# Macaron block on one Trainium2 core: the w2 products of the first expert pass move between two units of a projected tile

## The chip, the cores and the metric

One core of one Trainium2 chip. The metric is the device time of one execution in microseconds (us). The kernel before took 2403.8 us, the median of 3 runs (2402.45 to 2406.37).

## The reference

x has 8 batches of 1024 tokens of width 512. The block is a feed-forward half, an attention and the same feed-forward half again:

```
x = x + 0.5 * ffn(layernorm(x))
x = x + attn(layernorm(x))
x = x + 0.5 * ffn(layernorm(x))
```

ffn: 32 experts with a hidden width of 2048. Every expert picks 8 tokens of each batch by its gate weights and merges them into one row per batch, so an expert sees only 8 rows:

```
merged = einsum('bked,bke->bed', tok, vals)
h = gelu(concat([merged, 1]) @ w1[e])      # 512+1 -> 2048
o = concat([h, 1]) @ w2[e]                 # 2048+1 -> 512
out.at[flat_idx].add(einsum('beo,bke->bkeo', o, vals))
```

attn: q, k, v are projections of the normalised x by Wq, Wk, Wv (512 x 512 each); exp(q) and exp(k) enter a linear attention with running sums over the sequence, and Wo projects the result. All is float32. One expert has 8 MB of weights, so a pass over 32 experts reads some 270 MB.

## The kernel before, in words

Each engine has an instruction stream of its own, written out by hand, and they meet in semaphores: `wait_ge` stands ahead of the instruction that needs something, `then_inc` behind the one that gives it. The stages are: the gate over 64 tiles of 128 tokens (`gate_*`), the first expert pass (`experts_*` with p = 0), the attention (`attention_*`), the second expert pass (p = 1), and the final scatter.

**The first expert pass** does two things. For each expert e, TensorE (`experts_pe`, L733) runs the products with w1 (L738 to L746, into PSUM bank 0), transposes the result (L762 to L765, bank 1), and runs the products with w2 (L775 to L783, bank 4 or 5). Each weight matrix comes as two chunks of 2 MB: chunks 4e and 4e+1 are w1, 4e+2 and 4e+3 are w2. The products are thin (32 columns of stationary data, four side by side). Between them TensorE computes the projections of q, k and v of the first x ahead of the attention (`ahead_pe`, L918): tile 2e-1 behind the w1 products, tile 2e behind the transposes. A tile has three **units** (q, k, v), each 12 products of 128x512 into bank 2 or 3 in turn; the values are split in two parts (XTH, XTL and WTH, WTL), so one unit is 4 x 3 products. A unit may start when the unit two before it has been read out of its bank: q and k by ScalarE (L950, semaphore `s_pea`), v by VectorE (L959, `s_ped`). Every fourth expert TensorE also runs `scatter_pe` (two products) behind the w1 products.

**From transposes to w2 products.** VectorE adds the bias to the transposed values (L842, `s_hb`), ScalarE applies the gelu (L814, `s_ht`), and the w2 products wait for `s_ht` (L773). In `experts_act` (L800) the order for an expert is: copy of the w1 result (L806), `ahead_act` of tile 2e-1, gelu, `ahead_act` of tile 2e; every fourth expert then copies the sum of four experts from bank 4 or 5 (L826, `s_pt`), which `scatter_pe` waits for. `ahead_act` (L941) splits the next tile (L909), stores the tile before (`store_act`, L936, 768 KB to p_scratch on ScalarE's DMA queue), and reads the q and the k unit out of their banks. In `experts_dve` (L831) the order is the eviction of the v unit of tile 2e-1 (L959), the bias (L842), the split of the next tile (L915), the v unit of tile 2e.

**The weights** come through SyncE's queue (`experts_sp`, L715; `load_chunk`, L671). In the first pass they have four slots in SBUF, one for each chunk of an expert (`slot_of`, L239). The load of chunk g+4 waits until the products have used chunk g (`s_used`, raised behind the products at L746 and L783), and SyncE issues in the order of the chunks. Behind the four loads of every even expert it issues one load of 1 MB of xt_scratch (`load_xg`, L705), which holds the values that the projections read.

The first expert has an order of its own: its tile 0 is projected behind its w2 products (L785). In the second pass there are eight slots and no projections.

Of the kernel before, what the change touches and what calls it, by code (L numbers as in the profile page):

```python
# [20 lines left out]
def macaron_block(nc, x, Wq, bq, Wk, bk, Wv, bv, Wo, bo, gate_w, gate_b, w1, w2, out):  # L21
# [21 lines left out]
    with ctx:  # L43
# [195 lines left out]
        def slot_of(g):  # L239
            return g % 4 if g < 4 * E else (4, 5, 6, 7, 2, 0, 1, 3)[g % 8]  # L240
# [55 lines left out]
        def mm(o, l, r, start, stop):  # L296
            return nc.tensor.matmul(o, l, r, start=start, stop=stop, skip_group_check=True)  # L297
# [435 lines left out]
        def experts_pe(pe, p):  # L733
            pe.wait_ge(s_mg, 8 * p + 8)
            for e in range(E):
                x, g = E * p + e, 4 * (E * p + e)
                pe.wait_ge(s_hg, x)
                for kt in range(4):  # L738
                    h = g + kt // 2
                    v = ring[slot_of(h)].rearrange("p (k n) -> p k n", k=2)  # L740
                    pe.wait_ge(d_ring[slot_of(h)], 16 * turn[h])
                    for j in range(4):
                        t = mm(ps[32 * j:32 * j + 32, 0, :], MG[:, kt, 8 * e:8 * e + 32],
                               v[:, kt % 2, 512 * j:512 * j + 512], kt == 0, kt == 3)
                    if kt % 2 == 1:
                        t.then_inc(s_used, 1)  # L746
                if e == 0:
                    pe.wait_ge(d_b1, 64 * p + 64)
                    for q in range(4):
                        t = nc.tensor.transpose(ps[:, 1, 128 * q:128 * q + 128],  # L750
                                                BS.rearrange("p (c t) -> p t c", t=4)[:, q, :], IDN[:, :])
                    t.then_inc(s_btT, 1)
                if e % 4 == 0 and e:
                    scatter_pe(pe, p, e // 4 - 1)
                if p == 0 and e == 0:
                    weights_pe(pe, 2, 8)
                if p == 0 and e:
                    ahead_pe(pe, 2 * e - 1)
                pe.wait_ge(s_hg, x + 1)
                pe.wait_ge(s_hb, x)  # L760
                pe.wait_ge(s_bt, p + 1)
                for q in range(4):  # L762
                    t = nc.tensor.transpose(ps[:, 1, 128 * q:128 * q + 128],  # L763
                                            HG[e % 2].rearrange("p (c t) -> p t c", t=4)[:, q, :], IDN[:, :])
                t.then_inc(s_htT, 1)  # L765
                if p == 0 and e == 0:
                    weights_pe(pe, 8, 16)
                    bias_pe(pe)
                if p == 0 and e:
                    ahead_pe(pe, 2 * e)  # L770
                if e % 4 == 0:
                    pe.wait_ge(s_pt, x // 4 - 1)
                pe.wait_ge(s_ht, x + 1)  # L773
                k = 4 + e // 4 % 2
                for j in range(4):  # L775
                    h = g + 2 + j // 2
                    v = ring[slot_of(h)].rearrange("p (j i n) -> p j i n", j=2, i=4)
                    pe.wait_ge(d_ring[slot_of(h)], 16 * turn[h])
                    for q in range(4):
                        t = mm(ps[32 * q:32 * q + 32, k, :], HT[e % 4][:, 128 * q + 32 * j:128 * q + 32 * j + 32],  # L780
                               v[:, j % 2, q, :], e % 4 == 0 and j == 0, e % 4 == 3 and j == 3)
                    if j % 2 == 1:
                        t.then_inc(s_used, 1)  # L783
                if p == 0 and e == 0:
                    ahead_pe(pe, 0)  # L785
                if p == 1 and 1 <= e < 3:
                    rank_pe(pe, e - 1)
            scatter_pe(pe, p, 7)
            if p == 0:
                ahead_pe(pe, NT - 1)  # L790

        def scatter_pe(pe, p, G):
            pe.wait_ge(s_selc, 17)
            pe.wait_ge(s_pt, 8 * p + G + 1)
            for half in range(2):
                off = 128 * half + 28 - 4 * G
                t = mm(ps[:, 6 + half, :], SEL[:, off:off + 128], PT[G % 2], G == 0, G == 7)
            t.then_inc(s_sel, 1)
# [65 lines left out]
        def weights_pe(pe, lo, hi):  # L864
            for u in range(lo, hi):
                m, kt = u // 4, u % 4
                pe.wait_ge(*((d_wst[m], 16) if m < 2 else (d_x0[m - 2], 32)))
                if u == 2:
                    pe.wait_ge(s_pr3, 8)
                if u == 3:  # L870
                    pe.wait_ge(s_mg, 8)
                pe.wait_ge(s_wth, u - 3)
                pe.wait_ge(s_wtl, min(u - 3, 12))
                for o in range(4):
                    t = nc.tensor.transpose(ps[:, WB[u % 4], 128 * o:128 * o + 128],
                                            WST[m][:, o, 128 * kt:128 * kt + 128], IDN[:, :])
                t.then_inc(s_wT, 1)

        def bias_pe(pe):
            pe.wait_ge(s_wth, 16)  # L880
            pe.wait_ge(d_bias, 16 * 11)
            for g in range(4):
                t = mm(ps[:, 2, :], BVT[:, g:g + 1].broadcast_to([128, 128]), WO[:, g, :], g == 0, g == 3)
            t.then_inc(s_bo, 1)
# [30 lines left out]
            tt(XTL[t % 2], XG[h % 2][:, :, 128 * (t % 4):128 * (t % 4) + 128], XTH[t % 2].bitcast(F),  # L915
               ALU.subtract).then_inc(s_xsl, 1)

        def ahead_pe(pe, t):  # L918
            if t == 0:
                pe.wait_ge(s_bo2, 1)  # L920
            pe.wait_ge(s_xsl, t + 1)
            for u in range(3):
                q = 3 * t + u
                o = q - 2
                if o >= 0:
                    if o % 3 < 2:
                        pe.wait_ge(s_pea, o // 3 * 2 + o % 3 + 1)
                    else:
                        pe.wait_ge(s_ped, o // 3 + 1)
                for j in range(4):  # L930
                    mm(ps[:, 2 + q % 2, :], XTH[t % 2][:, j, :], WTH[u][:, j, :], j == 0, False)
                    mm(ps[:, 2 + q % 2, :], XTH[t % 2][:, j, :], WTL[u][:, j, :], False, False)
                    t_ = mm(ps[:, 2 + q % 2, :], XTL[t % 2][:, j, :], WTH[u][:, j, :], False, j == 3)
                t_.then_inc(s_pu, 1)
# [490 lines left out]
        def rank_pe(pe, h):  # L1425
            pe.wait_ge(s_rank, 14)
            pe.wait_ge(s_own, 7 * h + 1)
            for i in range(2):
                t = mm(ps[:, 2 + i, :], EARLIER, PICK[:, 512 * i:512 * i + 512], True, True)
            t.then_inc(s_cnt, 1)  # L1430
# [102 lines left out]
        @block.tensor  # L1533
        def _(eng):
            pe = Engine(eng)
            gate_pe(pe)
            experts_pe(pe, 0)
            attention_pe(pe)
            experts_pe(pe, 1)
            final_pe(pe)  # L1540
# [22 lines left out]
```

## Time and profile before

| | |
|---|---|
| median of 3 runs | 2403.8 us (2402.45 to 2406.37) |
| the profiled execution's own time | 2402.62 us |
| its span, first to last instruction | 2400.9 us |
| TensorE busy | 84% of the span |
| VectorE, ScalarE, GpSimd busy | 31%, 34%, 27% |
| DMA | 762 MB, mean 317 GB/s |
| granted TensorE clock, mean | 0.921 |

The span is what the views of the trace cover; the profiled execution's own time is 1.7 us longer. The gate runs until about 140 us, the first expert pass until about 980 us, the attention until about 1740 us, the second pass until about 2370 us. In the views, PE is TensorE's matmul, SPq is SyncE's queue of DMA issues, and L297 is a helper through which nearly all matmuls go, so groups are told apart by tiles and shapes: `ps<-big 128*32 128x512` is a thin expert product, `ps<-wth,xth`, `ps<-wtl,xth` and `ps<-wth,xtl` are the projections, L763 the transposes between w1 and w2. One thin float32 product has two records, so the w1 or the w2 products of an expert are 32 records.

### The profile page before, as it was taken

To read this page: it belongs to the slowest core of one execution; us is meant where nothing else is said; L and a number is where in the kernel's file an instruction comes from. 1 tells how busy PE (TensorE), PEld (TensorE's weight loads), DVE (VectorE), ACT (ScalarE), POOL (GpSimd) and SP (SyncE) were. 2 spreads that over 40 slices of the span, in tenths; PEclk is the share of its full clock that TensorE was granted. 3 is DMA by queue.
4 is the path that set the end of the run, shared out by engine and by line. 5 is a ranking of instruction groups with operands and counts; after the bars stand their busy time and mean duration, and the time that the engine had idled before them with its cause. 6 is when DMAs were issued, how large, how long until landed. Compare 5 with 4: busy or idle time off the path is not lost.

```text
span 2400.9 us, 44276 instructions
## 1 busy us (share of the span) xinstructions
PE 2027.0 (84%) x18716; PEld 1187.7 (49%) x18716; DVE 733.1 (31%) x1229; ACT 822.0 (34%) x1539; POOL 646.4 (27%) x803
## 2 busy tenths in 40 slices
PE   5789999999999999889999999999775666666555
PEld 4556566566656665666666666666521111111111
DVE  6631111111111111266777677677420000000002
ACT  6731111111111111257777777777500000000000
POOL 8510000000000000067777777777411000000002
PEclk9899999999999999999999999999887777777888
DMA  9989999999999999654545454544399999999995
GB/s 373 339 343 368 390 403 390 384 400 380 420 400 404 392 399 386 210 212 155 160 144 168 147 157 148 164 141 159 134 400 422 425 424 424 425 424 424 425 424 212
DMA packets 130709, 762.22 MB, mean 317 GB/s; under 512 B 21156, under 2 KB 21156, under 8 KB 77264
## 3 DMA queue, kind: packets, MB, share of 16 engines
q1 hardware_dynamic: 118736, 701.35, 74.3%
q10 hardware_dynamic: 9216, 50.34, 5.0%
q0 software_dynamic: 2560, 7.70, 0.8%
q8 instruction: 149, 2.44, 0.4%
q14 instruction: 48, 0.39, 0.0%
HBM read 648.09 MB, written 105.91 MB: 314 GB/s over the span
## 4 chain that ended last, share of the span: by engine, by line
PE 44%; DMA 38%; POOL 8%; ACT 4%; issue 3%; DVE 3%; POOLq 0%; SPq 0%; ACTq 0%; DVEq 0%
PE ps L297 40%; DMA big<-in_L_ffn_w 37%; PE ps L301 3%; POOL s L1397 1%; POOL big L1394 1%; POOL big L1368 1%; POOL big L1399 1%; ACT big L1237 1%; ACT ps L1221 1%; DVE big L627 1%; POOL s L1379 1%; DVE big L305 1%; POOL big L665 1%; POOL big L1361 1%; PE ps L427 0%
## 5 line engine op out<-in xcount | busy, mean ns | idle before, releaser
L297 PE MATMUL ps<-big 128*32 128x512 f32 (+5 forms) x13776 | 1009.7, 424 | 264.8 <-DMA big<-in_L_ffn_w 233.9
L297 PEld LDWEIGHTS ps<-big 128*32 128x32 f32 (+2 forms) x13776 | 384.3, 128 | 808.7 <-issue 399.9
L305 DVE TENSOR_TENSOR big<-ps,big 128x128 f32<-128x128 f32 (+3 forms) x373 | 338.1, 932 | 749.1 <-PE ps L763 570.0
L297 PE MATMUL ps<-wth,xth 128*128 128x512 f32 x768 | 310.2, 404 | 0.0
L806 ACT COPY big<-ps 128x512 f32<-128x512 f32 x64 | 37.5, 586 | 768.5 <-PE ps L297 768.5
L297 PE MATMUL ps<-wth,xtl 128*128 128x512 f32 x768 | 300.3, 391 | 0.0
L297 PE MATMUL ps<-wtl,xth 128*128 128x512 f32 x768 | 300.3, 391 | 0.0
L1386 POOL TENSOR_SCALAR big<-big 128x1 f32<-128x1 f32 x64 | 12.2, 190 | 903.9 <-ACT ps L1221 898.6
L297 PE MATMUL ps<-wo,s 128*128 128x512 f32 x768 | 211.1, 410 | 3.4 <-ACT big L1285 1.9
L301 PE MATMUL ps<-big 128*128 128x128 f32 x1032 | 167.4, 296 | 28.6 <-ACT big L575 12.4
L950 ACT ACTIVATE big<-ps,big 128x512 f32<-128x512 f32 x128 | 88.2, 689 | 262.0 <-PE ps L297 260.1
L959 DVE TENSOR_SCALAR big<-ps,big 128x512 f32<-128x512 f32 x64 | 48.1, 751 | 425.2 <-PE ps L297 425.2
L297 PEld LDWEIGHTS ps<-wth,xth 128*128 128x128 f32 x768 | 145.7, 190 | 56.1 <-issue 27.7
L301 PEld LDWEIGHTS ps<-big 128*128 128x128 f32 x1032 | 121.6, 149 | 103.2 <-issue 60.7
L1485 POOL DMA_INDIRECT out_x<-big,idx x16 | 15.8, 987 | 553.5 <-DVE big L1479 548.7
L297 PEld LDWEIGHTS ps<-wtl,xth 128*128 128x128 f32 x768 | 145.5, 189 | 30.0 <-issue 1.9
L297 PEld LDWEIGHTS ps<-wth,xtl 128*128 128x128 f32 x768 | 144.8, 189 | 31.2
L297 PEld LDWEIGHTS ps<-wo,s 128*128 128x128 f32 x768 | 135.5, 190 | 28.3 <-ACT big L1285 3.8
L305 DVE TENSOR_TENSOR xtl<-big,xth 128x512 fp32r<-128x512 f32 x64 | 44.2, 692 | 305.6 <-ACT xth L909 305.6
L297 PE MATMUL ps<-s,tri 128*128 128x512 f32 x240 | 101.7, 471 | 11.6 <-ACT s L1246 7.0
L1394 POOL TENSOR_TENSOR big<-big 128x512 f32<-128x512 f32 x64 | 82.1, 1283 | 59.4 <-ACT big L1237 59.4
L1379 POOL TENSOR_TENSOR s<-big,s 128x512 fp32r<-128x512 f32 x64 | 82.6, 1290 | 10.4 <-ACT s L1281 4.3
(124 smaller groups left out, 1777.6 us busy)
## 6 DMA issues: line engine op xcount, KB each, us to landing
big<-in_L_ffn_w SPq DMA_DIRECT2D x256, 2048.0 KB, 22.0
p_scratch<-big ACTq DMA_DIRECT2D x64, 768.0 KB, 10.0
big<-p_scratch SPq DMA_DIRECT2D x64, 768.0 KB, 5.5
big<-in_L_attn_x SPq DMA_DIRECT2D x68, 256.0 KB, 2.9
xt_scratch<-big SPq DMA_DIRECT2D x16, 1024.0 KB, 8.2
big<-xt_scratch SPq DMA_DIRECT2D x16, 1024.0 KB, 15.5
x_weight_scratch<-big SPq DMA_DIRECT2D x64, 256.0 KB, 3.3
out_x<-big SPq DMA_DIRECT2D x64, 256.0 KB, 3.4
```

Source lines behind the costliest of these rows:

```text
L297: return nc.tensor.matmul(o, l, r, start=start, stop=stop, skip_group_check=True)
L301: t = nc.tensor.transpose(ps[:, k, 128 * j:128 * j + 128], src[:, 128 * j:128 * j + 128], IDN[:, :])
L305: return nc.vector.tensor_tensor(o, p, q, op)
L627: nc.vector.bn_stats(ST6[j], XLA[h % NX4][:, j, :]).then_inc(s_bst4, 1)
L665: nc.gpsimd.tensor_scalar(X[:, j, :], X[:, j, :], MV_[:, j, 0:1], RS_[:, j:j + 1], ALU.subtract, ALU.mult).then_inc(s_nmp, 1)
L806: nc.scalar.copy(HG[e % 2], ps[:, 0, :]).then_inc(s_hg, 1)
L950: nc.scalar.activation(PST[t % 2][:, u, :], ps[:, 2 + q % 2, :], ACT.Identity, scale=STD[:, t:t + 1]).then_inc(s_pea, 1)
L959: nc.vector.tensor_scalar(PST[t % 2][:, 2, :], ps[:, 2 + q % 2, :], STD[:, t:t + 1], None, ALU.mult).then_inc(s_ped, 1)
L1221: nc.scalar.activation(ps[:, 7, :], X1[m % 4], ACT.Square, bias=SX1[m % 2], scale=-float(D), accum_out=SQ1[m % 2]).then_inc(s_x1sq, 1)
L1237: nc.scalar.activation(PB[m % 4][:, 0, :], PB[m % 4][:, 0, :], ACT.Exp, scale=RS[m % 2]).then_inc(s_qe, 1)
L1379: nc.gpsimd.tensor_tensor(ATL, AT, ATH.bitcast(F), ALU.subtract).then_inc(s_atl, 1)
L1394: nc.gpsimd.tensor_tensor(PB[j][:, 0, :], PB[j][:, 0, :], BK, ALU.mult).then_inc(s_qb, 1)
```

## The change

Of tile 2e, whose three units stood between the transposes and the w2 products of expert e (e from 1 to 31), only the first unit (q) is left there. The second and the third (k and v) are issued behind the w2 products. Tile 2e-1, expert 0 with its tile 0, the second pass, and all other engines' streams are untouched.

```
@@ experts_pe
                 if p == 0 and e:
-                    ahead_pe(pe, 2 * e)
+                    ahead_pe(pe, 2 * e, (0,))
                 if e % 4 == 0:
                     pe.wait_ge(s_pt, x // 4 - 1)
                 pe.wait_ge(s_ht, x + 1)
...
-                if p == 0 and e == 0:
-                    ahead_pe(pe, 0)
+                if p == 0:
+                    ahead_pe(pe, 2 * e, (1, 2) if e else (0, 1, 2))
                 if p == 1 and 1 <= e < 3:
                     rank_pe(pe, e - 1)
@@
-        def ahead_pe(pe, t):
+        def ahead_pe(pe, t, units=range(3)):
             if t == 0:
                 pe.wait_ge(s_bo2, 1)
             pe.wait_ge(s_xsl, t + 1)
-            for u in range(3):
+            for u in units:
                 q = 3 * t + u
```

## Rows read from the trace of the kernel before

**Rows 1.** The page: span, DMA share in tenths and GB/s of 40 slices

```profile
span 2400.9 us, 44276 instructions
...
DMA  9989999999999999654545454544399999999995
GB/s 373 339 343 368 390 403 390 384 400 380 420 400 404 392 399 386 210 212 155 160 144 168 147 157 148 164 141 159 134 400 422 425 424 424 425 424 424 425 424 212
```

**Rows 2.** Waits of PE, 230 to 1000 us: total us, times, longest

```profile
PE ps L297 <- DMA big<-in_L_ffn_w: 37.0, 14, 3.0
...
PE ps L297 <- ACT big L826: 0.7, 1, 0.7
```

**Rows 3.** The chain that ended last: start us, us, what (first, middle, last)

```profile
215.78 25.23 DMA big<-in_L_ffn_w
...
694.18 24.83 DMA big<-in_L_ffn_w
...
905.95 24.93 DMA big<-in_L_ffn_w
```

**Rows 4.** Timeline of PE, 686 to 760 us: start us, us, what, count, idle before

```profile
687.04 7.07 PE L297 MATMUL ps<-big 128*32 128x512 f32 x64
...
711.10 5.36 PE L297 MATMUL ps<-big 128*32 128x512 f32 x48
719.05 2.84 PE L297 MATMUL ps<-big 128*32 128x512 f32 x16 [2.60 <-DMA big<-in_L_ffn_w]
...
739.60 7.07 PE L297 MATMUL ps<-big 128*32 128x512 f32 x64
```

**Rows 5.** Windows: us, engines busy, granted clock, DMA share, GB/s

```profile
692.00:739.00 47.00, 44.41 (x234) 30.54 (x227) 5.42 (x9) 9.36 (x16) 0.00 (x0) 0.96 1.01 422
241.00:931.00 690.00, 655.90 (x3672) 421.61 (x3676) 80.19 (x130) 125.20 (x214) 0.00 (x0) 0.98 0.96 396
...
1800.00:2300.00 500.00, 310.20 (x1728) 72.62 (x1728) 8.46 (x37) 26.14 (x56) 8.99 (x9) 0.77 1.01 424
```

**Rows 6.** Timeline of SyncE's queue: issues of loads near two block boundaries

```profile
689.03 0.38 SPq L18 DMA_DIRECT2D big<-in_L_ffn_w  x1
...
692.46 0.34 SPq L18 DMA_DIRECT2D big<-in_L_ffn_w  x1
...
721.94 0.34 SPq L18 DMA_DIRECT2D big<-in_L_ffn_w  x1
```

**Rows 7.** GB/s in 40 slices of 0.5 us: 680 to 700, 732 to 752 us

```profile
GB/s 459 492 360 360 459 471 344 422 573 307 504 324 455 389 389 143 45 25 0 0 197 115 328 442 377 442 426 410 442 426 410 459 426 279 344 262 344 422 385 426
...
GB/s 393 393 459 524 426 426 307 512 299 438 496 348 504 377 426 393 258 102 37 25 0 131 164 311 393 492 393 393 442 442 426 410 426 377 360 360 246 348 397 393
```

**Rows 8.** Timeline, 701 to 706 us: transposes, bias, gelu, first projection product

```profile
702.34 0.63 PE L763 MATMUL ps<-big 128*128 128x128 f32 x4
702.73 0.48 PE L297 MATMUL ps<-wth,xth 128*128 128x512 f32 x1
...
703.21 0.28 DVE L305 TENSOR_TENSOR big<-ps,big 128x128 f32<-128x128 f32 x1
703.53 0.31 ACT L814 ACTIVATE big<-big 128x128 f32<-128x128 f32 x1 [3.02 <-DVE big L305]
```

**Rows 9.** DMA issues and total, 241 to 931 us: count, KB each, us to landing

```profile
DMA packets 31039, 273.26 MB, mean 396 GB/s; under 512 B 2704, under 2 KB 2704, under 8 KB 9360
...
big<-in_L_ffn_w SPq DMA_DIRECT2D x104, 2048.0 KB, 19.6
p_scratch<-big ACTq DMA_DIRECT2D x52, 768.0 KB, 10.1
```

**Rows 10.** Timeline of PE: an expert with the scatter products; an uncut short block

```profile
658.31 5.36 PE L297 MATMUL ps<-big 128*32 128x512 f32 x48
666.39 3.84 PE L297 MATMUL ps<-big 128*32 128x512 f32 x20 [2.73 <-DMA big<-in_L_ffn_w]
...
975.55 3.64 PE L297 MATMUL ps<-big 128*32 128x512 f32 x32
```

More of the change, by code:

```diff
@@ L769, in experts_pe @@
                 if p == 0 and e:
-                    ahead_pe(pe, 2 * e)
+                    ahead_pe(pe, 2 * e, (0,))
                 if e % 4 == 0:
@@ L783, in experts_pe @@
                         t.then_inc(s_used, 1)
-                if p == 0 and e == 0:
-                    ahead_pe(pe, 0)
+                if p == 0:
+                    ahead_pe(pe, 2 * e, (1, 2) if e else (0, 1, 2))
                 if p == 1 and 1 <= e < 3:
@@ L916, in split_dve, with ahead_pe @@
                ALU.subtract).then_inc(s_xsl, 1)
-        def ahead_pe(pe, t):
+        def ahead_pe(pe, t, units=range(3)):
             if t == 0:
@@ L921, in ahead_pe @@
             pe.wait_ge(s_xsl, t + 1)
-            for u in range(3):
+            for u in units:
                 q = 3 * t + u
```

## The prediction

> **What bounds the kernel now.** I read the page first, then the waits of PE, the chain that ended last, and last the timelines and the DMA slices of one pair of experts. In the page the DMA engines are nearly full from the start of the first expert pass to its end, but move 380 to 420 GB/s there, where the second pass moves 424 [rows 1]. The reader is to see a resource that is almost, not quite, the bound. In the waits, PE stands still in this pass for one thing that counts: 14 waits for a weight chunk, 37.0 us together [rows 2]. The chain shows them at a fixed distance: from 215.78 to 905.95 us there are 13 steps, so one every 53.09 us, which is once in two experts [rows 3]. I call two experts a pair; 14 pairs have such a wait.
>
> The timeline of PE gives what a pair is made of [rows 4]. Blocks of thin products (w2 of one expert, then w1 of the next, 64 records) begin at 687.04, 711.10 and 739.60. The first expert of the pair takes 24.06 us and waits for nothing. In the second the last 16 records (the second w1 chunk) come 2.60 us late, and the expert takes 28.50 us. Of its 4.44 us excess 2.60 are the wait; the other 1.84 are slower products just behind it (16 records take 2.84 us where 64 take 7.07). The engine had been idle for those 2.6 us, and the granted clock of the stretch that holds the wait is 0.96, so part of it ran at 1.2 instead of 2.4 GHz [rows 4, 5].
>
> Why is the chunk late? It was issued at 694.18 and landed 24.83 us later [rows 3], behind all that SyncE had issued just before it: w2 chunks from 689.03 on, the xt load, w1 at 692.46 [rows 6]. All loads of an expert are issued in one burst, since w2 and w1 products stand side by side on PE and their slots come free together. And before each burst the queue runs dry: in the slices of 0.5 us the rate falls to 0 at 689 and at 742 us, once per pair [rows 7]. Summed over the 8 low slices, the first hole is worth 3.0 us at 424 GB/s (the rates 143, 45, 25, 0, 0, 197, 115, 328 lack 5.99 slices), the second 2.8 us. Between holes DMA moves 422 GB/s, over the whole stretch 396 [rows 5]. **So the pass loses DMA time because slots come free too late, and PE pays for it a little later.**
>
> **The change part by part.** Nothing is added or removed: the same 24 products per expert stand behind the w2 products instead of ahead of them.
>
> *Earlier slots.* A unit takes (711.10 - 702.73) / 3 = 2.79 us [rows 4, 8]. The w2 products run two units, 5.6 us, earlier, so both w2 slots come free 5.6 us earlier, and their loads (and the xt load behind them in SyncE's queue) are issued at about 683.4 instead of 689.03. That is 4 us before the rate begins to fall at 687.5 [rows 7]. The w1 slots come free as before. The hole closes: 2.8 us per pair by the slices. Two bounds: a smaller one of 1.2 us, if most of the low slices are 16 DMA engines that finish unevenly and do so without a hole as well; and the whole pass's shortfall, 53.09 x (1 - 396/422) = 3.3 us [rows 5]. I take 2.8, because the slices show the hole itself. Then a pair takes 53.09 - 2.8 = 50.3 us by DMA. The byte count agrees: 273.26 MB in 13 pairs are 21.0 MB each, at 422 GB/s 49.8 us [rows 5, 9].
>
> *PE's own floor.* It must stay under 50.3. Without a wait and without slow products a pair is 2 x 24.06 = 48.12 us. The scatter products come in every second pair: from 666.39 to 687.04 are 20.65 us, where the same stretch without them would be 24.06 - 5.29 = 18.77 (24.06 less the 48 records ahead of the wait, which end 5.29 us after their start), so 1.9 us, or 0.95 per pair [rows 4, 10]. The block of 64 is now two blocks of 32. An uncut 32 takes 3.64 us, so two take 0.21 us more than one of 64 [rows 4, 10]; with the resumed projection I say 0.3 per expert, between 0 and 0.6, and 0.6 per pair. Floor: 48.12 + 0.95 + 0.6 = 49.7 us. PE is under DMA by 0.6 us: DMA still sets the pace, and what is late next is again the second w1 chunk, by a fraction of what it was. The 1.84 us of slow products lie inside the 53.09, so they are not counted a second time.
>
> *Bytes and other queues.* ScalarE's stores of 768 KB (52 in the stretch, 10.1 us to land) keep their places, one behind the copy of w1's result, one behind the gelu [rows 9]. They come to lie beside other loads of the same sum. Nothing.
>
> *The gelu's cover.* The w2 products wait for bias and gelu. The transposes start at 702.34, the gelu ends at 703.84 [rows 8]; before, three units stood in between, now one, until 702.73 + 2.79 = 705.5. The cover is still 1.7 us. Nothing; if that cover were gone, each us would cost 31 us.
>
> *ScalarE's order.* `ahead_act` of tile 2e reads unit k out of its bank, and now waits for it through the w2 products, 3.6 us longer. Queued behind it are the copy of the four-expert sum (L826) and the copy of the next w1 result. Unit v and the w1 products still run after unit k, some 6 us, so both copies are in time. The store of the tile before is issued ahead of that wait. Nothing. At the end of the pass the scatter no longer waits 0.7 us for L826 [rows 2], as two units now cover it: 0.7 gained.
>
> *Sum.* 14 pairs x 2.8 + 0.7 = 39.9 us, less 31 x 0.3 us only where PE and not DMA is the bound (the first three experts: 1 us). About 39 us, all ahead of the attention, which starts earlier by as much and is bound by its own chain. The profiled execution took 2402.6 us, so 2363.6; the median of the three runs is 1.2 us above it. I say 2364 us.
>
> One rule of the Trainium skill would put the DMA side elsewhere. Rows first: over 47 us without a hole this kernel moves 422 GB/s, and 424 over 500 us of the second pass [rows 5]. The page "DMA: Bandwidth & Descriptors", section "Anatomy of one DMA", gives a fixed part of some 2.0 us and bytes at 436 GB/s. By it (an estimate from that page) the 21.0 MB of a pair would need 48.2 us, DMA would be under PE, and the sum would end at PE's floor, which is rival 2. Its fixed part agrees with the hole: an issue at 689.03, the rate back at 690 to 691 us [rows 6, 7].
>
> **The rivals.**
> 1. *DMA was full anyway* (gains little or nothing). Its share reads 0.96 over the pass, and closing a hole cannot return more than that. If the low slices are mostly uneven ends of 16 engines, and PE's cut blocks take 0.6 us each, a pair falls to 51.9 or so: 14 x 1.2 + 0.7 = 17 us, 2386 us. For it: the bursts' ragged rates of 300 to 500 [rows 7]. Against it: two slices at 0. With the chunk as late as before and its wait unchanged, nothing would be gained: 2403 us.
> 2. *PE becomes the bound.* The DMA engines catch up entirely, waits and slow products go, and a pair takes PE's floor: 14 x (53.09 - 49.7) + 0.7 = 48 us, 2355 us; without the cost of cut blocks 57 us, 2346 us. For it: it is only 0.6 us away.
> 3. *Slower: the gelu is no longer covered.* Its place is the wait of L773. It decides once transposes, bias and gelu together take more than the one unit: they take 1.5 us from the first transpose against 3.2 us of cover. VectorE does the bias behind the eviction of unit v, ScalarE the gelu behind that of unit k, so a late eviction could push it. The gain is used up when the wait exceeds 39 / 31 = 1.3 us per expert, that is from a chain of 4.5 us on; at 5 us the kernel would be slower by 31 x 1.8 - 39 = 17 us, 2420 us. Against it: all links are measured and none moves.
> 4. *The change doesn't do what it says*: loads of w2 are issued earlier only if SyncE isn't held by something ahead. Ahead of them stand the two w1 loads, issued two tiles earlier. It is not held. 2404 us.
>
> **How the numbers follow.** Chances: forecast, DMA-bound pairs of 49.9 to 51 us, 0.62; rival 2 0.14; rival 1 with a small gain 0.13, with none (and rival 4) 0.04; rival 3 and anything else slower 0.07. A measurement of this kernel can tell about 0.2%, 5 us. Faster by more: 0.62 + 0.14 + 0.13 = 0.89, rounded to 0.88; same 0.05; slower 0.07. The range holds the forecast, rival 2 with half the cost of the cuts and rival 1's small gain: 2350 to 2386 us.
>
> **What would show it.** In the waits of PE the 37.0 us for chunks should shrink to under 15, in shorter waits. The rate over the pass should rise from 396 to about 418 GB/s, no 0.5 us slice of it near 0. The chain's step should be about 50.3 us for a pair. A w2 load should be issued some 5.6 us before the unit that used to precede it ends. No wait for L814 should appear. The granted clock of the pass should be at or above 0.98. It is wrong if the holes stay, if PE waits for w2 chunks instead, or if the pass shortens but the attention begins no earlier.

## The result and the profile after

The changed kernel takes 2359.1 us (median of 4 runs, 2357.39 to 2363.23) against 2403.1 us before (4 runs): a ratio of 0.9819, 95% interval 0.9803 to 0.9834, 44.0 us less. A second measurement on another occasion gave 0.9814 (0.9799 to 0.9830). The forecast was 2364, with a range of 2350 to 2386.

The profiled execution is the slowest of the four, 2363.2 us with a span of 2361.4. Its page, to be held against [rows 1]:

```profile
span 2361.4 us, 44276 instructions
...
DMA  9989999999999998364545454543699999999994
GB/s 373 334 340 404 417 427 420 423 426 418 427 421 421 425 421 340 118 223 152 157 147 162 147 161 148 156 155 127 220 402 424 425 424 425 424 425 424 425 424 180
```

From 236 to 885 us each slice now moves 417 to 427 GB/s, where the second pass moves 424; before it was 380 to 420. The slices at the start of the pass (340 and 404 GB/s) are lower, as they were before. The windows view says more (us, engines busy, granted clock, DMA share, GB/s), beside [rows 5]:

```profile
241.00:887.00 646.00, 646.00 (x3664) 413.85 (x3664) 80.17 (x130) 124.54 (x214) 0.00 (x0) 1.00 1.01 422
```

PE is busy for 646.00 of 646 us at the full granted clock, and DMA moves at the same time what it moved before only between two holes. The waits of PE from 230 to 900 us list nothing at all, where 14 waits for weights took 37.0 us [rows 2]. The DMA slices of 241 to 887 us, each 16 us long:

```profile
DMA  9999999999999999999999999999999999999999
GB/s 428 389 426 430 421 427 432 406 424 428 421 427 430 411 420 429 424 427 424 411 433 414 426 427 425 412 427 423 426 429 421 411 425 422 428 427 423 420 417 423
```

An expert on PE's timeline (start, us, what) is to be read against [rows 4]:

```profile
375.18 0.63 PE L763 MATMUL ps<-big 128*128 128x128 f32 x4
378.50 3.64 PE L297 MATMUL ps<-big 128*32 128x512 f32 x32
387.73 3.64 PE L297 MATMUL ps<-big 128*32 128x512 f32 x32
399.60 0.63 PE L763 MATMUL ps<-big 128*128 128x128 f32 x4
```

The block of 64 records has become two of 32: w2 at 378.50, w1 at 387.73, with the k and v units between them. From one group of transposes to the next are 24.42 us. And SyncE's queue, against [rows 6]:

```profile
455.48 2.10 SPq L18 DMA_DIRECT2D big<-in_L_ffn_w  x2
457.67 0.96 SPq L18 DMA_DIRECT2D big<-xt_scratch  x1
464.71 2.04 SPq L18 DMA_DIRECT2D big<-in_L_ffn_w  x2
466.43 0.33 SPq L18 DMA_DIRECT2D big<-in_L_ffn_w  x1
```

The two w2 loads and the xt load go out at 455.48 to 457.67, the two w1 loads from 464.71 (the last line is the second of them, from a narrower window). From the first w2 issue to the last w1 issue are now 10.95 us; before they were 694.18 - 689.03 = 5.15 us [rows 3, 6]. I call this distance the **head start** of the w2 loads; the experiments turn on it.

### The profile page after: what moved, and what is told of

It is laid out like the page before. It is cut to its first block, busy times and chain, and to the rows that moved or that the text cites. A ratio compares the mean times of both kernels' runs of the same rounds, so it can differ in the third digit from the quotient of the medians.

```text
span 2361.4 us, 44276 instructions
## 1 busy us (share of the span) xinstructions
PE 2017.2 (85%) x18716; PEld 1181.1 (50%) x18716; DVE 733.2 (31%) x1229; ACT 821.3 (35%) x1539; POOL 646.7 (27%) x803
## 4 chain that ended last, share of the span: by engine, by line
PE 58%; DMA 24%; POOL 8%; ACT 4%; issue 4%; DVE 3%; POOLq 0%; SPq 0%; ACTq 0%; DVEq 0%
PE ps L297 53%; DMA big<-in_L_ffn_w 24%; PE ps L301 3%; POOL s L1397 1%; POOL big L1394 1%; POOL big L1368 1%; POOL big L1399 1%; ACT big L1237 1%; PE ps L763 1%; ACT ps L1221 1%; DVE big L627 1%; POOL big L665 1%; POOL big L1361 0%; DVE big L305 0%; PE ps L427 0%
## 5 line engine op out<-in xcount | busy, mean ns | idle before, releaser
L297 PE MATMUL ps<-big 128*32 128x512 f32 (+5 forms) x13776 | 997.7, 419 | 230.5 <-DMA big<-in_L_ffn_w 206.4
L301 PE MATMUL ps<-big 128*128 128x128 f32 x1032 | 168.8, 298 | 28.2 <-ACT big L575 12.6
## 6 DMA issues: line engine op xcount, KB each, us to landing
big<-in_L_ffn_w SPq DMA_DIRECT2D x256, 2048.0 KB, 19.5
```

Source lines behind the costliest of these rows:

```text
L301: t = nc.tensor.transpose(ps[:, k, 128 * j:128 * j + 128], src[:, 128 * j:128 * j + 128], IDN[:, :])
```

## The experiments

To compare passes I take the start of the transposes (the 0.63 us group above) of expert 3 and of expert 27 and divide by 12: the time of a pair. For the changed kernel:

```profile
225.19 0.63 PE L763 MATMUL ps<-big 128*128 128x128 f32 x4
...
821.67 0.63 PE L763 MATMUL ps<-big 128*128 128x128 f32 x4
```

That is 49.71 us; the kernel before has 223.94 and 861.22, so 53.11. All the experiments in one table (medians; "kernel before" was 2401.9 to 2403.2 beside each of them; PE's waits for weights in the profiled execution, from 230 us to 900, for before to 1000 and for the last three to 960 us):

```
                   us      ratio (95% interval)     pair us  waits us, times  head start us
before           2403.1   1                         53.11    37.0, 14          5.2
after            2359.1   0.9819 (0.9803, 0.9834)   49.71    none             11.0
late_loads       2464.4   1.0253 (1.0235, 1.0270)   56.54    60.8, 30          2.0
late_loads_k     2377.6   0.9895 (0.9879, 0.9912)   51.13    15.9, 13          6.3
one_unit         2359.8   0.9819 (0.9803, 0.9836)   49.90     2.3, 3           8.2
all_units        2388.1   0.9937 (0.9921, 0.9954)   51.62    22.8, 25 (gelu)
fewer_products   2343.7   0.9758 (0.9735, 0.9781)   49.48    98.6, 43
less_xt          2356.8   0.9814 (0.9793, 0.9836)   49.71    none
fewer_less       2320.0   0.9663 (0.9642, 0.9684)   47.75    94.9, 41
before_less_xt   2374.8   0.9882 (0.9858, 0.9906)   50.88    19.5, 13
before_xt_behind 2371.5   0.9863 (0.9845, 0.9882)   50.71    17.5, 15
after_xt_behind  2359.6   0.9817 (0.9801, 0.9832)   49.71    none
after_again      2359.7   0.9814 (0.9799, 0.9830)   49.71    none
```

### Is it the time of the issue? late_loads, late_loads_k

PE's order stays that of the changed kernel; only SyncE is held back, in `load_chunk`:

```
             if before[g] is not None:
                 sp.wait_ge(s_used, before[g] + 1)
+            if 8 < g < 4 * E and part >= 2:
+                sp.wait_ge(s_used, 4 * e + 1)
```

> PE's order is that of the changed kernel; only the issue of the w2 loads is held back on SyncE until the first w1 chunk of the next expert is used, which is where the kernel before had it. Theory (the gain is the earlier issue, which keeps the DMA queue from running dry): the hole in the DMA rate is back once per pair, PE waits again some 2.5 us for the second w1 chunk in 14 places, and the time is 2395 to 2408 us. Rival (the new order helps on PE itself, for instance by a better spread of its work or fewer slow products): it stays near the changed kernel, 2357 to 2366 us.

late_loads_k waits for the k unit instead: `sp.wait_ge(s_pu, 3 * (2 * (e - 1)) + 2)`.

> As late_loads, but the w2 loads are held back only until the k unit behind the w2 products is done, so they come 2.8 us later than in the changed kernel and some 4.6 us earlier than in late_loads. Theory: the queue still holds work when they are issued (the hole before began 1.5 us ahead of the issue, and this issue is 2.8 us ahead of that one), so at most a small dip, no waits of PE over 0.5 us, and 2358 to 2370 us. Rival (the gain goes in proportion to how early the loads are): half of it, 2375 to 2385 us.

With PE's order unchanged and nothing but the issue delayed, the whole gain goes, so it hangs on the issue; the rival of late_loads is out. But late_loads overshoots the theory by 56 us, and late_loads_k, at 2377.6, lies outside the theory's range and inside the rival's (2375 to 2385): 26 us of the gain, where "nearly all" and "half" were the two guesses. Whether the gain goes in proportion to the distance is left to one_unit. The issues tell why both missed. late_loads (timeline of SyncE's queue, then one line of the chain of waits: start, us, what):

```profile
442.23 0.89 SPq L18 DMA_DIRECT2D big<-in_L_ffn_w  x2
443.22 0.41 SPq L18 DMA_DIRECT2D big<-xt_scratch  x1
443.67 1.00 SPq L18 DMA_DIRECT2D big<-in_L_ffn_w  x2
...
444.24 28.37 DMA big<-in_L_ffn_w
```

I had taken this to be the kernel before. It isn't: all five loads are issued within 2.0 us, where before the first w2 load was 5.15 us ahead of the last w1 load. The last w1 chunk lands 28.37 us after its issue instead of 24.83, and PE waits in every expert, not in every second (30 waits). The DMA slices of 0.5 us from 460 to 480 us show the hole before the next burst, at 470 us:

```profile
GB/s 389 643 426 360 328 492 459 426 393 393 426 492 492 426 360 426 393 524 459 426 197 33 0 33 0 131 98 393 393 377 426 459 360 459 459 377 459 393 328 377
```

And late_loads_k (timeline of SyncE's queue, first w2 and last w1 issue), with its line of PE's waits:

```profile
468.83 1.17 SPq L18 DMA_DIRECT2D big<-in_L_ffn_w  x2
...
475.10 0.33 SPq L18 DMA_DIRECT2D big<-in_L_ffn_w  x1
...
PE ps L297 <- DMA big<-in_L_ffn_w: 15.9, 13, 2.0
```

Its head start is 6.3 us, and 13 waits of 1.2 us are left.

These give a rule that I had not had. I call the time from one group of transposes to the next without waits (24.06 us before, 24.42 after) PE's period. In the heavy half (the one with the xt load) a burst that starts on an empty queue needs 30.0 us from the first w2 issue to the landing of the last w1 chunk (694.18 + 24.83 - 689.03 before; 30.4 in late_loads). PE needs that chunk one PE period less half a block after its issue: 24.06 - 1.8 = 22.3 us before, 24.42 - 1.8 = 22.6 us after. So PE doesn't wait if the head start is at least 30.0 - 22.6 = 7.4 us. What it lacks is the wait. For the kernel before, 30.0 - 22.3 - 5.15 = 2.6 is no test, since all its terms come from the pair whose wait is 2.60. late_loads_k tests it: 30.0 - 22.6 - 6.3 = 1.1, measured 1.2 on average. For late_loads it gives 30.4 - 22.6 - 2.0 = 5.8; in the heavy half at 467 us two waits in a row, 2.96 and 1.23 us, and 16 slower records between them (3.64 us instead of 1.8) make 6.0. The changed kernel, at 10.95, should wait for nothing, and does. The 7.4 us themselves were not measured: 6.3 still waits, and one_unit, next, lies on the other side.

### Other distances: one_unit, all_units

one_unit leaves q and k ahead of the w2 products and moves v alone:

```
-                    ahead_pe(pe, 2 * e, (0,))
+                    ahead_pe(pe, 2 * e, (0, 1))
...
-                    ahead_pe(pe, 2 * e, (1, 2) if e else (0, 1, 2))
+                    ahead_pe(pe, 2 * e, (2,) if e else (0, 1, 2))
```

> Only the v unit stands behind the w2 products; q and k stand ahead of them. The slots come free 2.8 us earlier than before instead of 5.6 us. Theory: as late_loads_k, the hole is closed or nearly so and PE's floor is the same (the blocks are cut just as often): 2358 to 2370 us. Rival (in proportion): 2375 to 2385 us.

2359.8 us: within the noise the whole gain with half the distance, so a gain in proportion is out. Its head start is 8.2 us, above 7.4 (the w2 loads at 509.27, the second of the two w1 loads some 1.7 us behind 515.79), and PE waits 2.3 us in all, in three heavy halves, where the rule has no wait (why these three bursts land later is open); its pair is 0.2 us longer than the changed kernel's:

```profile
509.27 2.10 SPq L18 DMA_DIRECT2D big<-in_L_ffn_w  x2
511.47 0.69 SPq L18 DMA_DIRECT2D big<-xt_scratch  x1
515.79 2.04 SPq L18 DMA_DIRECT2D big<-in_L_ffn_w  x2
...
PE ps L297 <- DMA big<-in_L_ffn_w: 2.3, 3, 1.1
```

all_units moves all three (the call of `ahead_pe` between transposes and w2 products goes, the one behind them projects the whole tile), so nothing covers bias and gelu.

> All three units of tile 2e stand behind the w2 products, so nothing covers bias and gelu. Theory (PE is at its floor in the changed kernel, each us on it costs 31): PE waits some 1.1 us per expert for the gelu, 31 x 1.1 = 34 us, so 2385 to 2398 us, with waits of PE for ACT L814 of 30 us or more. Rival (DMA sets the pace, PE has room): the wait is absorbed for the most part, 2358 to 2370 us.

2388.1 us, as the theory said. The timeline (start, us, engine, what, idle before) shows the uncovered chain, which was hidden in [rows 8]:

```profile
460.66 0.63 PE L763 MATMUL ps<-big 128*128 128x128 f32 x4
...
461.53 0.28 DVE L305 TENSOR_TENSOR big<-ps,big 128x128 f32<-128x128 f32 x1
461.85 0.31 ACT L812 ACTIVATE big<-big 128x128 f32<-128x128 f32 x1 [3.02 <-DVE big L305]
...
462.21 2.35 PE L297 MATMUL ps<-big 128*32 128x512 f32 x20 [0.91 <-ACT big L812]
```

PE stands idle for 0.91 us per expert, 28 us in 31 experts, and the kernel is 28.9 us slower than the changed one. Nothing of it is absorbed: each us on PE costs a us. The table's 22.8 us in 25 waits are those of 230 to 900 us; from 140 to 1010 us there are 28.2 us in 31, where I had expected 30 or more.

### Which of the two is the bound? fewer_products, less_xt, fewer_less

fewer_products leaves out the product of XTH and WTL for tiles 1 to 62, so those projections lack a correction term; less_xt loads a quarter of XG from the third load on, so the projections of those tiles partly use old values; fewer_less does both.

```
                 for j in range(4):
                     mm(ps[:, 2 + q % 2, :], XTH[t % 2][:, j, :], WTH[u][:, j, :], j == 0, False)
-                    mm(ps[:, 2 + q % 2, :], XTH[t % 2][:, j, :], WTL[u][:, j, :], False, False)
+                    if t == 0 or t == NT - 1:
+                        mm(ps[:, 2 + q % 2, :], XTH[t % 2][:, j, :], WTL[u][:, j, :], False, False)
```

```
-            sp.dma_start(XG[h % 2], xtd[h]).then_inc(d_xgl[h % 2], 16)
+            n = 4 if h < 2 else 1
+            sp.dma_start(XG[h % 2][:, 0:n, :], xtd[h][:, 0:n, :]).then_inc(d_xgl[h % 2], 16)
```

> The changed kernel, with the product of the high part of x with the low part of the weights left out for tiles 1 to 62 (a third of the projection products, 24 per expert, 5.4 us of PE per expert); every load and store stays. Theory A (PE sets the pace of the changed kernel, DMA has next to no room behind it, its bytes need 49.7 us per pair against PE's 49.7): the pass stays at 49.6 to 50.3 us per pair, PE waits for weights some 10 us per pair, total 2350 to 2366 us. Rival B (DMA has room, as 436 GB/s would give it, 48.2 us per pair): 20 us faster, 2335 to 2342 us.

> The changed kernel, with three quarters of each load of xt_scratch left out from the third on (0.79 MB less per pair, 1.9 us of DMA); the projections then use old values. Theory A (PE is the bound): no gain, 2355 to 2363 us, the DMA rate falls to some 406 GB/s. Rival B (DMA is the bound): 14 x 1.9 = 26 us faster, 2332 us.

> Both at once: fewer products on PE and less xt to load. Theory A (each of the two bounds stands right behind the other): now the pass shortens by DMA's share, 47.8 us per pair, some 24 us less than fewer_products: 2326 to 2342 us. If a third thing bounded the pass (the issue of loads, a latency of slots), it would stay within 8 us of fewer_products.

The same window, 241 to 841 us, of the three in this order:

```profile
241.00:841.00 600.00, 514.29 (x2849) 282.81 (x2851) 75.67 (x123) 117.11 (x202) 0.00 (x0) 0.93 1.01 426
```

```profile
241.00:841.00 600.00, 600.00 (x3403) 383.24 (x3396) 74.71 (x121) 116.28 (x200) 0.00 (x0) 1.00 1.00 407
```

```profile
241.00:841.00 600.00, 518.48 (x2978) 291.23 (x2977) 78.74 (x128) 121.67 (x210) 0.00 (x0) 0.97 1.01 426
```

Taking DMA work away leaves the pair at 49.71 us to the last digit, and the rate falls to 407 GB/s: PE is the bound of the changed kernel. Taking a fifth or more of PE's work away shortens the pair only to 49.48 us, at 426 GB/s and with PE waiting 98.6 us: DMA stands 0.23 us behind PE. Only both together bring 47.75 us. The total of fewer_products, 2343.7, is below the theory's range though its pair is only 0.1 us under what it said. The first experts, ahead of the stretch that I had counted, are half of its 15 us: expert 3's transposes start at 217.41 instead of 225.19 us. fewer_less misses its range by 6 us, and its transposes of expert 3 start at 216.37.

The page of the Trainium skill that I weighed in the prediction, "DMA: Bandwidth & Descriptors", section "Anatomy of one DMA", has bytes at 436 GB/s and a fixed part of some 2.0 us. With PE waiting for weights the trace shows 426 GB/s and 49.48 us for a pair, where the page's figure gave an estimate of 48.2; the measurement decides. The section is on DMAs that GpSimd issues, where these loads are issued by SyncE, which the prediction left out. It also puts most of the fixed part behind the last byte, so the 1 to 2 us from the issue at 689.03 to the return of the rate [rows 6, 7], which the prediction took for an agreement, are another thing and confirm nothing.

### The same cure without PE: before_less_xt, before_xt_behind, after_xt_behind, after_again

before_less_xt is the kernel before with the smaller xt loads.

> The kernel before, with the same three quarters of the xt loads left out. By the theory its pair is made of DMA's bytes plus a hole: the w1 chunk lands 1.9 us earlier, PE's wait falls from 2.6 to about 0.7 us, and the slow products behind it go too, so up to 14 x 3.7 = 52 us and at least 14 x 1.9 = 26 us: 2352 to 2377 us, with the hole in the DMA rate longer than before (4 us and more). If the hole were no loss (uneven ends of the engines only), nothing but the bytes would go: 2377 us.

2374.8 us, at the weak end. The hole is there and long where it comes (560 to 580 us in slices of 0.5 us; it lacks 5.4 us at 424 GB/s):

```profile
GB/s 406 426 537 360 393 492 393 393 262 373 410 442 258 94 111 119 37 25 0 0 0 0 16 197 66 508 311 475 377 426 492 328 492 492 311 344 295 328 295 373
```

So the bytes were saved and part of them went into a longer hole. The waits shrink to 19.5 us in 13, 1.5 us each (0.9 to 2.3), where I had expected 0.7. The rule gives 28.3 - 22.3 - 5.15 = 0.8 for the burst issued at 466.97 us (its last w1 chunk is issued at 472.12 and lands 23.12 us later), whose wait is 0.89; it doesn't say why the others are longer.

before_xt_behind leaves PE's order as it was and has SyncE issue the xt load behind the two w1 loads instead of ahead of them:

```
                         load_chunk(sp, g + ahead)
-                if p == 0 and e % 2 == 0 and 2 <= e // 2 + 1 < NT // 4:
-                    load_xg(sp, e // 2 + 1)
+                    if p == 0 and e % 2 == 1 and g % 4 == 1 and 2 <= e // 2 + 1 < NT // 4:
+                        load_xg(sp, e // 2 + 1)
```

> The kernel before, with PE's order untouched; SyncE issues the xt load behind the two w1 loads of the even expert instead of ahead of them. The runs so far say that PE doesn't wait if the w2 loads are issued ahead of the last w1 load by at least the time from the first w2 issue to the landing of the last w1 chunk (30.0 us in the heavy half, with the xt load) less one PE period without the last half block (22.3 to 22.6 us), that is by 7.4 us; before it was 5.2. Here the 30.0 us lose the xt load's 2.5 us, so the threshold falls to 4.9 and 5.2 is just enough. That theory: waits of PE under 8 us in all, a pair of 49.1 (PE's floor with uncut blocks) to 50.3 us, 2352 to 2368 us, with no change of PE's order. Rival (the hole at the block's start costs what it cost, wherever the xt load stands, since all w2 and w1 loads still come in one burst): 2385 to 2403 us.

2371.5 us, 31.7 us faster than before, and between the two expectations. Its window and its waits:

```profile
241.00:841.00 600.00, 584.75 (x3328) 381.75 (x3317) 73.26 (x119) 115.23 (x197) 0.00 (x0) 1.00 1.00 417
...
PE ps L297 <- DMA big<-in_L_ffn_w: 17.5, 15, 3.0
```

Most of the gain can be had on SyncE alone, which confirms that PE's order was only the means. But 15 waits of 1.2 us remain, where under 8 us in all were expected, so the rule fails here. It counts the heavy half alone, and here the xt load lies ahead of the next w2 loads. That its bytes now delay the following expert's chunks too is my reading; no run tests it.

> The changed kernel with the xt load moved in the same way. It is at PE's floor of 49.7 us per pair and waits for nothing, so this changes nothing: 2356 to 2363 us. If DMA were what holds it, it would fall below 2353 us.

> The changed kernel once more, to stand beside the two others and to see whether the 4 us that its profiled execution lost behind the last expert come again: 2357 to 2361 us, and if they were chance the last transposes to the end take 42 to 45 us instead of 46.

Both as expected in time: 2359.6 and 2359.7, pairs of 49.71. The 4 us behind the last expert did come again; the section on the hardware has them. No version that does the whole work beat the changed kernel by more than a measurement can tell (fewer_products and fewer_less are faster, but leave work out).

## Why the prediction was right, and where it wasn't

**The time and its cause.** 2359 against a forecast of 2364: 44 us of gain against 39. (The sum as written, 2363.6 and 1.2, is 2364.8.) The account of the cause held where runs tested it: slots that come free too late (late_loads), a hole once per pair, which closes, a burst whose last chunk PE waits for. That nothing else on ScalarE or VectorE became a wait is shown by the empty list of PE's waits, and what the gelu's cover is worth by all_units, where its loss costs 28.9 us for 0.91 us per expert; the prediction had priced it at 31 us per us of wait.

**The pace.** Here a term was mis-sized. I said that DMA sets the pace at 50.3 us a pair and PE lies 0.6 us under it. It is the other way: PE sets it at 49.71 us, and DMA could do 49.48 (fewer_products). The step that failed is "I take 2.8, because the slices show the hole itself". Of the three values in that step the upper bound was right: the whole pass's shortfall of 3.3 us, which would have given 49.8, and so was the byte count of 49.8, which I called agreement though it was 0.5 us off. I had summed only the 8 low slices. Against 424 GB/s the whole 20 us of each line of [rows 7] lack 3.6 and 3.4 us, some 0.6 of them behind the hole, and the pair became 3.4 us shorter. With 3.4 in place of 2.8 DMA is no longer above PE's floor. So what happened is rival 2, to which I gave 0.14: PE becomes the bound, waits and slow products go. The forecast that the second w1 chunk would still be late, by a fraction, failed with it: PE waits for no chunk.

**PE's floor** was put at 49.7 us and measured at 49.71, though its terms were less exact: the cut block costs 24.42 - 24.06 = 0.36 us per expert (0.3 said), the scatter products 26.15 - 24.42 = 1.73 us (1.9 said; with an expert 26.15 us from transposes to transposes every fourth time).

**The forecast time came out closer than its pace.** In the profiled executions the last transposes of the pass start at 966.96 - 921.25 = 45.7 us earlier (chain of waits), near rival 2's 48. At the end of the span 39.5 are left. The last wait for a weight chunk of the second pass is for a load issued 2327.24 - 2283.69 = 43.5 us earlier, so some 2 us went between and 4 behind it (in these executions). The medians keep 44.0. Rival 2's 2355 us assumed that all of it is kept. That the forecast missed by 5 us and not by 9 is luck: losses that it had not foreseen made up for half of what it had too little.

```profile
921.25 0.47 PE ps L763 x4
...
2283.69 38.97 DMA big<-in_L_ffn_w
```

**"What would show it"**: waits under 15 us (none), 418 GB/s (422), clock at or above 0.98 (1.00), no wait for the gelu (none). In slices of 0.5 us around three bursts (450 to 470, 476 to 496 and 498 to 518 us) the rate never falls below 274 GB/s. The attention begins earlier: its first copy L1002 in the chain starts at 964.22 instead of 1010.66 us, so 46.4 us, which are the pass's 45.7 and the 0.7 of the scatter. The pair's step of 50.3 us was wrong by 0.6.

## What to carry to other kernels

Where a queue of loads is nearly full but not quite, look at slices shorter than a period for the holes, and ask which slot's release ends each of them. Loads that are released together are issued together, and the last of them pays for all; spreading the releases, by moving covered work between two consumers or by moving a load that nobody awaits to the end of the burst, needs no more buffers. How far to move is set by a threshold (burst time less the consumer's period), and beyond it more distance gives nothing; keep enough cover for the chain that stood under the moved work.

The Trainium skill, page "Perfetto Trace Analysis", section "Optimization Strategy", says that a gap which repeats on the engine that should be saturated can mean too few buffers. The 14 waits, of 2.1 to 3.0 us, fit that, as there are four slots for four chunks; but with the same four slots the time at which they come free (one_unit) gave the whole gain, and the order of the loads in the queue (before_xt_behind) most of it.

## What the runs showed of the hardware that I had not expected

*Two resources near their limit at once.* PE is busy in 646.00 of 646 us and DMA at 422 GB/s in the same stretch, with neither slowing the other to be seen: the k and the v unit between the two blocks take 387.73 - 378.50 - 3.64 = 5.59 us, 2.80 each, as a unit did before (2.79). At 407 GB/s (less_xt) the pair is the same 49.71 us, and where PE has room (fewer_products) the rate is only 426.

*A wait is not always followed by slow products.* In the kernel before, the 10 us behind ten of the 14 waits have a granted clock of 0.70 to 0.86; behind the other four (454.84, 615.33, 666.39 and 878.19 us), with waits of 2.82, 2.09, 2.73 and 2.86 us, it stays at 1.00. The prediction's 1.84 us of slower products are those of one pair; over the pass they are 53.11 - 2 x 24.06 - 0.87 (scatter) - 2.65 (wait) = 1.5 us. What decides between the two is open.

*The end depends on the clock.* The last scatter of the second pass, four records behind a wait for weights, takes 3.78 us in the profiled execution of the changed kernel and 1.98 in that of less_xt, whose order of instructions there is the same (and 1.98 before). The granted clock is 0.50 in the one and 1.00 in the other. The products behind it run at one pace in both, 7.10 us for 64 records and 9.64 for 88. First the changed kernel, then less_xt:

```profile
2327.06 3.78 PE L297 MATMUL ps<-big 128*128 128x512 f32 x4 [0.70 <-ACT big L826]
```

```profile
2323.17 1.98 PE L297 MATMUL ps<-big 128*128 128x512 f32 x4 [0.71 <-ACT big L827]
```

In the second pass PE is busy in 60 to 62% of the time, at a granted clock of 0.77 (before) to 0.81 (after). Of the 4 us that the changed kernel loses against the kernel before behind the last wait for weights, 1.8 are this scatter and 1.7 the 16 w2 records ahead of it (3.69 us against 1.97); half a us is open. From the last transposes to the end there were 41.9 to 46.7 us in the 13 profiled executions, and the three with the changed kernel's order and full loads had 45.6 to 46.7 of them. Why their scatter is slow and less_xt's is not was not tried and stays open.
